# The last two steps of an attention loop in another order, with the next stage's first load a step earlier

## What is computed

```python
x = x + _L0_xattn_ref(_layernorm(x), ctx_1024, Wq, Wk, Wv, Wo, gq, gk)   # 16 heads of 128
x = x + _L0_ffn_ref(_layernorm(x), W1, b1, W2, b2, W3, b3)               # 512 -> 1024 -> 1024 -> 512
x = x + _L1_xattn_ref(_layernorm(x), ctx_1024, pos, pos, Wq, Wkv, Wout, bout)   # 32 heads of 16
x = x + _L1_ffn_ref(_layernorm(x), W_q, keys, down_embed, up_embed, gate_w, up_w, down_w)
```

```python
# _L1_xattn_ref: 16 tiles of 128 rows, each with its own 128 context rows
q = rope(x @ Wq, pos); k, v = split(ctx @ Wkv); k = rope(k, ctx_pos)
w = softmax(einsum('bqhd,bkhd->bhqk', q, k) * scale)
return einsum('bhqk,bkhd->bqhd', w, v).reshape(b, n, 512) @ Wout + bout
# _L1_ffn_ref: top 8 of 1024 experts a row by two halves of keys, beside a gated product
queries = (x @ W_q).reshape(2, n, 64); routing = einsum('tnd,tdk->tnk', queries, keys)
ew = silu(einsum('nh,nkh->nk', x, down_embed[indices])) * softmax(scores)
return silu(x @ gate_w) * (x @ up_w) @ down_w + einsum('nk,nkh->nh', ew, up_embed[indices])
```

## Time and profile before

| | |
|---|---|
| median of 3 runs | 1950.87 us (1949.71 to 1953.98) |
| the profiled execution | 1948.46 us, span 1946.7 us |
| PE busy | 1886.3 us, 97% of the span |
| DVE, ACT, POOL busy | 65%, 38%, 28% |
| granted PE clock, mean | 0.99 |
| DMA | 212.43 MB, mean 109 GB/s |

### The profile page before, as it was taken

One profiled execution on the slowest core, in us unless ns is written; L12 is line 12 of the kernel. 1 busy time (PEld: TensorE's weight loads), 2 busy tenths in 40 slices (PEclk: granted clock), 3 DMA queues, 4 the chain that ended last, 5 costly groups with the idle time before them and its releaser, 6 DMA issues. The chain is left out here.

```text
span 1946.7 us, 35580 instructions
## 1 busy us (share of the span) xinstructions
PE 1886.3 (97%) x13040; PEld 1538.1 (79%) x13040; DVE 1274.3 (65%) x2493; ACT 747.5 (38%) x2307; POOL 552.5 (28%) x702
## 2 busy tenths in 40 slices
PE   6999999999999999999999899998799999999999
PEld 5788888778888878888888677776688888888887
DVE  6666656765665655434254688886468878888786
ACT  5545555655555542211121455555332222122211
POOL 4333322222224325211021434333110222322321
PEclk9999999999999999999999999999899999999999
DMA  6453333544345433111022211112122545654554
GB/s 203 131 158 78 91 76 82 149 101 116 96 124 143 120 114 99 49 43 54 11 79 87 76 44 47 45 50 73 37 92 67 194 163 191 202 194 166 193 170 157
DMA packets 165654, 212.43 MB, mean 109 GB/s; under 512 B 29104, under 2 KB 117168, under 8 KB 165552
## 3 DMA queue, kind: packets, MB, share of 16 engines
q1 hardware_dynamic: 141840, 124.08, 23.1%
q0 software_dynamic: 23712, 87.04, 13.4%
HBM read 140.80 MB, written 17.56 MB: 81 GB/s over the span
## 5 line engine op out<-in xcount | busy, mean ns | idle before, releaser
L2421 POOL DMA_INDIRECT m_ring<-in_table,m_row x128 | 126.6, 989 | 371.4 <-DVE l_x_all L2534 265.6
L48 PE MATMUL four_banks<-l_yT_hi,m_hi 128*128 128x512 f32 x512 | 199.4, 389 | 0.0
L48 PE MATMUL four_banks<-l_yT_lo,m_hi 128*128 128x512 f32 x512 | 199.2, 389 | 0.0
L533 ACT ACTIVATE prob<-four_banks,mx,rms 128x128 f32<-128x128 f32 x256 | 121.6, 581 | 171.2 <-DVE mx L671 171.2
L1149 DVE TENSOR_SCALAR f_relu<-bank,f_b 128x512 f32<-128x512 f32 x64 | 47.9, 749 | 162.5 <-ACT f_h_hi L1092 162.4
L1092 ACT ACTIVATE f_h_hi<-bank,f_b 128x512 fp32r<-128x512 f32 x64 | 44.1, 689 | 255.1 <-PE bank L48 255.1
L335 POOL TENSOR_TENSOR rms<-ssq,constants 128x4 f32<-128x4 f32 x128 | 27.3, 214 | 394.5 <-ACT junk_k L521 277.4
L338 POOL TENSOR_TENSOR rms<-rms,constants 128x4 f32<-128x4 f32 x128 | 129.8, 1014 | 10.1
L48 PEld LDWEIGHTS four_banks<-l_yT_hi,m_hi 128*128 128x128 f32 x512 | 96.1, 188 | 20.1 <-issue 0.2
L48 PEld LDWEIGHTS four_banks<-l_yT_lo,m_hi 128*128 128x128 f32 x512 | 96.1, 188 | 19.9
L2398 ACT ACTIVATE m_act_of<-m_dot,l_ln_y 128x2 f32<-128x2 f32 x64 | 18.9, 296 | 240.6 <-DVE m_junk L2524 235.9
(11 more groups left out here) (312 smaller groups left out, 5224.6 us busy)
## 6 DMA issues: line engine op xcount, KB each, us to landing
qkT<-blocks SPq DMA_DIRECT2D x256, 128.0 KB, 2.7
pT_sb<-dealt SPq DMA_DIRECT2D x256, 64.0 KB, 2.1
f_stage<-in_w POOLq DMA_DIRECT2D x14, 512.0 KB, 4.7
f_x_in<-x SPq DMA_DIRECT2D x18, 256.0 KB, 3.2
ctx_in<-in_ctxT SPq DMA_DIRECT2D x32, 128.0 KB, 2.6
x_in<-in_x SPq DMA_DIRECT2D x16, 256.0 KB, 3.2
x<-xres SPq DMA_DIRECT2D x16, 256.0 KB, 2.9
l_rotB<-inverses SPq DMA_DIRECT2D x16, 256.0 KB
```

The lines of the kernel that those rows point to most:

```text
L48: mm = pe.matmul(out, st, mv, start=first and n == 0, stop=last and n == len(terms) - 1)
L533: a = act.activation(prob[g][:, j, :].rearrange("q (b a) -> q a b", b=4), scores, ACT.Exp, bias=mx[g][:, 1, j:j + 1], scale=rms[g][:, 0, j ...
L2421: pool.indirect_dma_start(ring[slot][:], None, table, bass.IndirectOffsetOnAxis(ap=row[:, tile_of(g), k:k + 1], axis=0)).then_inc(S[f"got{ ...
```

## The change

It moves pieces of steps 13 to 15 and of the tail; no arithmetic is added or left out.

- SP: the first load stands in step 13 behind `load_ctx(15)`, ahead of `move_maxima(14, 0)` and `store(12)`. `store(14)` goes behind `move_outputs(15)`.
- ACT: `ahead["scalar"](act, 0)` goes from the start of step 15 into step 14, ahead of `o_in(14, 1)`. `y_hi(12)` is first in step 15, `y_hi(13)` ahead of `exps(15, 1)`.
- DVE: in step 15 the splits go from the start to behind `y_lo(13)`; `y_lo(12)` is ahead of `invert(14)`, `y_lo(13)` ahead of `normalise(14)`. `spread(0)` goes from the end of step 15 behind `invert(15)`, and `layer_norm_y(14)` ahead of `normalise(15)`.
- PE: `turn_y(12)` is ahead of `score_shifted(15, 0)`; `turn_y(13)` and `route_queries(0)` are ahead of `score_shifted(15, 1)`; `mix(15)` is ahead of `output(14)`. For that it writes banks 7 and 4, not 7 and 6, and its waits and those of `output(15)` and `route_queries(1)` change.

```diff
@@ SP @@
             if there(s + 2):
                 load_ctx(sp, s + 2)
-            if there(s + 1):
-                move_maxima(s + 1, 0)
-            if there(s - 1):
-                store(s - 1)
             if isinstance(s, int) and s == NB - 3:
                 sp.wait_ge(*at("q_made", NB - 1))
                 ahead["first_load"](sp)
+            if there(s + 1):
+                move_maxima(s + 1, 0)
+            if there(s - 1) and there(s + 1):
+                store(s - 1)
...
         move_sums(NB - 1)
         move_outputs(NB - 1)
+        store(NB - 2)
         store(NB - 1)
@@ PE: mix, output, route_queries @@
+    def mix_bank(s, f):
+        return (7, 6 if there(s + 1) else 4)[f]
+
     def mix(pe, s):
         pe.wait_ge(*at("v_copied", s))
         pe.wait_ge(*at("exped1", s))
-        if there(s - 1):
+        if not there(s + 1):
+            pe.wait_ge(*at("yT_lo", SHORT + 1))
+        elif there(s - 1):
             pe.wait_ge(*at("y_added", s - 1))
...
         if there(s + 2):
             pe.wait_ge(*at("k_copied", s + 2))
+        elif there(s + 1):
+            pe.wait_ge(*at("o_in1", s))
         else:
-            pe.wait_ge(*at("o_in1", s))
+            pe.wait_ge(*at("y_added", s - 1))
...
         if c == 1:
-            pe.wait_ge(*at("yT_lo", SHORT + 1))
+            pe.wait_ge(*at("o_in1", NB - 1))
@@ PE: step @@
+            if last:
+                turn_y(pe, SHORT)
             if there(s):
                 score_shifted(pe, s, 0)
...
             if last:
-                turn_y(pe, SHORT)
+                turn_y(pe, SHORT + 1)
+                route_queries(pe, 0)
...
                 score_shifted(pe, s, 1)
             if last:
-                turn_y(pe, SHORT + 1)
-                route_queries(pe, 0)
+                mix(pe, s)
...
                 output(pe, s - 1)
...
-            if there(s):
+            if there(s) and not last:
                 mix(pe, s)
@@ ACT: o_in, step @@
-        act.activation(mixed_sb[:, f, :], bank[(7, 6)[f]][:], ACT.Copy).then_inc(S[f"o_in{f}"], 1)
+        act.activation(mixed_sb[:, f, :], bank[mix_bank(s, f)][:], ACT.Copy).then_inc(S[f"o_in{f}"], 1)
...
             if isinstance(s, int) and s == NB - 1:
-                act.wait_ge(*at("v_made", NB - 1))
-                ahead["scalar"](act, 0)
+                y_hi(act, SHORT)
...
             if isinstance(s, int) and s == NB - 1:
-                y_hi(act, SHORT)
+                y_hi(act, SHORT + 1)
...
                 exps(act, s, 1)
-            if isinstance(s, int) and s == NB - 1:
-                y_hi(act, SHORT + 1)
...
                 turned_in(act, s + 1, 1, 1)
+            if isinstance(s, int) and s == NB - 2:
+                act.wait_ge(*at("v_made", NB - 1))
+                ahead["scalar"](act, 0)
@@ DVE: step, tail @@
-            if isinstance(s, int) and s == NB - 1:
-                ahead["vector"](dve, 0)
             if there(s - 2):
                 layer_norm_y(dve, s - 2)
             if there(s + 2):
                 x_lo(dve, s + 2)
+            if isinstance(s, int) and s == NB - 1:
+                y_lo(dve, SHORT)
             if there(s - 1):
                 invert(dve, s - 1)
...
             if isinstance(s, int) and s == NB - 1:
-                y_lo(dve, SHORT)
+                y_lo(dve, SHORT + 1)
+                ahead["vector"](dve, 0)
...
-            if isinstance(s, int) and s == NB - 1:
-                y_lo(dve, SHORT + 1)
...
-            if isinstance(s, int) and s == NB - 1:
-                spread(dve, 0)
...
         invert(dve, NB - 1)
+        spread(dve, 0)
+        layer_norm_y(dve, NB - 2)
         normalise(dve, NB - 1)
-        layer_norm_y(dve, NB - 2)
         ahead["vector"](dve, 1)
```

More of the change, by code:

```diff
@@ L1630, in mix @@
                 for j in range(4):
-                    mm = pe.matmul(bank[(7, 6)[f]][PAD * j:PAD * (j + 1), t * P:(t + 1) * P], v_sb[:, 8 * t + 2 * j + f, :],
+                    mm = pe.matmul(bank[mix_bank(s, f)][PAD * j:PAD * (j + 1), t * P:(t + 1) * P], v_sb[:, 8 * t + 2 * j + f, :],
                                    probT[f][:, j, t, :], start=True, stop=True)
```

## The result

The changed kernel takes 1939.59 us (median of 5 runs, 1937.73 to 1942.84) against 1950.87 (5 runs, 1949.68 to 1953.98). The ratio is 0.9942, 95% interval 0.9931 to 0.9953: 11.3 us faster, 9.2 to 13.5. Forecast were 1943.9 us, 6.95 us faster, in a range that begins at 1940.3: right in direction, the gain too small by more than a third. Two further comparisons on other chips gave 0.9947 (0.9934 to 0.9961) and 0.9949 (0.9936 to 0.9961). The three together are 10.5 us, and 6.95 us (0.9964) lies outside each interval. The profiled execution took 1939.87 us with a span of 1938.1.

A forecast was written before the change was run, and what follows sets the result against it. PE bounds the kernel, so the gain is how much earlier `output(15)` starts: 8.35 + 0.5 - 0.3 - 0.6 - 1.0 = 6.95 us, from 1948.46 to 1941.5 profiled, 1943.9 as median; range 1940.3 to 1947.4.

The forecast's parts named there:

- part 1: Step 13: first load issued earlier on SP, so the sums of tile 13 go out sooner; gain 4.1 us.
- 0.9 us in each of two steps: SP loop: better store of the reciprocals if SP is held a little; used only for the likeliest case's range.
- is absorbed in the next: PE's waits: a clock fall starting at an earlier wait costs nothing; at `output(13)` or `output(14)` at most 2.4 us each.
- What bounds it: PE, busy 97% of the span; the change works only on about 1345 to 1405 us, the experts stage keeps the gain.
- The load behind the broadcast of tile 12, 0.3 us: Step 13: 1.5 MB issued right behind that broadcast slows it; cost 0.3 us, bounds 0 and 2.8.
- rival (a): Step 13: the load slows the broadcast of tile 12 by 2.8 us instead of 0.3; 1946.4 us, chance 0.13.
- `mix(15)` ahead of `output(14)`, 4.25 us: Step 15: mixing fills PE's wait, sums of tile 15 go out earlier; `mix(14)` to `output(15)` 28.8 us, gain 4.25 us.
- The tail, 0.5 us: After `output(15)`: full clock brings `turn_y(15)` earlier, limited by VectorE; gain 0.5 us, between 0 and 0.7.
- The clock, -1.6 us: PE clock falls cost 0.6 us at `output(13)` and 1.0 at `output(14)`, between 0 and 2.4 each.
- The maxima's write: Step 13: SP's `move_maxima(14,0)` may land up to 1 us later behind the load; `score_shifted(14,0)` has over a microsecond in hand.
- the likeliest case: Whole kernel: all parts work as summed; chance 0.68, range 1940.5 to 1946.5 us from clock terms and better reciprocal stores.
- its difference to the median, 2.4 us: Whole kernel: median of runs lies 2.4 us above the profiled execution; added to 1941.5 to give 1943.9 us.

The follow-up runs named there:

- the idle products: Kernel before, with unused products added in two of PE's waits, 20 ahead of `turn_k(15,0)` and 16 ahead of `output(15)`: ratio 0.9988, 2.3 us faster.

## Why the prediction was wrong

The prediction's own steps, in the profiles (us; two of the kernel before, three of the changed one; gains are differences of the means):

| stretch | before | changed | gain | forecast |
|---|---|---|---|---|
| `mix(12)` to `mix(13)` | 18.96, 18.56 | 18.87, 19.59, 19.43 | -0.5 | -0.3 |
| `mix(13)` to `mix(14)` | 23.23, 23.90 | 19.59, 19.54, 18.03 | 4.5 | 4.1 - 0.6 = 3.5 |
| `mix(14)` to `output(15)` | 33.11, 33.10 | 29.50, 29.54, 28.62 | 3.9 | 4.25 - 1.0 = 3.25 |
| `output(15)` to `turn_y(15)` | 11.20, 10.12 | 10.12, 10.12, 10.12 | 0.5 | 0.5 |
| `turn_y(15)` to the end | 530.15, 529.82 | 529.42, 529.66, 529.43 | 0.5 | 0 |
| together | | | 8.9 | 6.95 |

**The term that failed is the size of part 1, the load a step earlier: 4.1 us.** Its sum took 4.45 us from the odd copies to the broadcast, from the loop of tile 15. In its place in step 14 it took 3.05 us (1355.05 to 1358.10), and 3.04 to 3.05 in all ten profiles with the early load. With the load late, the same passage took 4.4 to 4.85 us in three of the four profiles and 3.07 in the fourth; what makes it short isn't shown. So the heads of tile 13 were ready 1.4 us earlier than in the sum. Where nothing else was late, the stretch took 18.0 us, as in the third profile: 5.2 to 5.9 us gained, not 4.1. Of the eight profiles with the early load and no idle products, six took 17.7 to 18.5 us. The prediction knew that this piece of the loop could be shorter (0.9 us in each of two steps) and kept it for the end of its range.

In the first two profiles another step of the prediction, wrong as well, hid that gain: that a fall of the clock "that starts at an earlier wait is absorbed in the next". The clock fell behind the wait of 1.99 us (the score products of L1616 at 1357.95 took 2.09 us, at 1372.16 at full clock 1.17). The next wait, 1 to 2.5 us ahead of `output(13)`, which should have absorbed it, was no longer there, since the heads came early. PE itself was late and reached `output(13)` 15.5 us after `mix(13)`; in the third profile it was 14.0, and by the sum 15.1.

The other steps:

- *What bounds it* was right: nearly all of the gain came out of 1350 to 1411, and the experts' stage kept it. The 0.5 us less from `turn_y(15)` to the end is in no step of the prediction. It is inside the spread of that stretch over all other versions (529.3 to 530.1 us), so it isn't shown to be the change's.
- *The load behind the broadcast of tile 12, 0.3 us*: from its issue to `normalise` 4.1 to 5.5 us in the ten profiles with the early load, mean 4.7, and 4.1 to 4.5 in the four without, mean 4.2. The price was small, about 0.5 us, and on the broadcast itself rival (a)'s 2.8 us was never reached. But in two of the ten, those of the late `spread(1)` and of the split put back, the late broadcast led to a wait of 1.7 and 1.8 us ahead of `output(12)` and the clock fell behind it; there `mix(13)` came 21.4 and 21.6 us after `mix(12)`, about what the rival had said, by another way.
- *`mix(15)` ahead of `output(14)`, 4.25 us*: from `mix(14)` to `output(15)` 28.6 us with `output(14)` at full clock, where the forecast had 28.8, and 29.5 with it at the low clock. Mechanism and size were right, the pieces less so: `output(14)` started 15.4 to 15.6 us after `mix(14)` instead of 15.0, and in the third profile the way from there was shorter by as much. Undone, it cost 6 to 7 us, not 4, because the undone state leaves longer waits than before (6.90 and 5.07 us).
- *The tail, 0.5 us*: right, and bounded by VectorE, as said: with `spread(1)` moved away it takes 8.8 us instead of 10.1.
- *The clock, -1.6 us*: against the third profile, the first two lost 1.5 us in step 14 and 0.9 behind `mix(14)`, on average over the three 1.6 us. That this equals the charge is luck: it was put on falls at `output(13)` (in none of the three) and at `output(14)` (in two). What the low clock cost the kernel before, which I had taken as all but hidden, stays open: 2.3 us by the idle products in time, with an interval from 0.6 to 4.1, and nothing by their profile.

Two smaller slips changed nothing. The maxima's write at 1347.78 was to land up to 1 us later behind the load; SP's next transfer, which waits for it, went out 3.3 us after it (1351.05), 1.9 us later than before (1347.32 to 1348.74), and PE still didn't wait. And the upper end of the likeliest case should have been 1947.1, not 1946.5: clock terms of 4.8 us instead of 1.6 take 3.2 us from the gain.

What stays open is the rest, why the timed runs give 10.5 us and the profiles 8.9. It may be no more than the spread. The profile on which the prediction rested (1948.46 us) lies below all of its 5 timed runs. I had carried its difference to the median, 2.4 us, over as a constant, which is right only if both kernels scatter alike; the first profile of the changed kernel lies 0.3 us above its median. The mean granted clock of the timed executions is 0.989 before and 0.992 after, and the clock and the time of before's executions go together (correlation -0.65 in 21 runs, about 1 us for 0.001). That points to the clock, but it isn't shown: the second profile of before has the same amount of low clock as the first, and the filled one much less without being faster.

## What to carry to other kernels

A large load belongs where nothing small stands behind it in the same queue: 1.5 MB ahead of a 16 KB transfer of sums cost 2.8 us there and 4 us at the end. When a loop's length is added up from pieces, look at all passages of a piece and not at one: what was taken as 4.45 us took 3.56 to 4.45 in the profile of before, and 3.05 after. And ask what a wait was hiding before you count on it: once the loop was shorter, the low clock that the wait would have absorbed cost 1.5 us in two of three profiles. When work is pulled forward into a wait, look at the wait that it leaves behind, and put something there too: without `mix(15)` in the gap the same moves were 6 to 7 us worse.

## What the runs showed of the hardware

- A store of 256 KB issued right behind a broadcast made its use 0.8 us later (4.46 against 3.68 us), although it was issued 0.7 us after. Over all profiles the broadcast of tile 15 took 4.2 to 4.5 us to `normalise` in the eight with the store behind it and 3.6 to 4.1 in the six without.
- The write of the reciprocals between four small copies is uneven: from the first copies to the broadcast it took 3.03, 3.05, 4.19, 4.45 and 4.81 us in the profiles, up to 5.15. Some 2.9 us of it are SP's own time to issue the five transfers (1.20, 0.57 and 1.14 us at 1355.05).
- After waits of about 2 us the granted clock fell at different places in executions of the same kernel. Behind the same 2.04 us `mix(15)` of the changed kernel took 1.96 us in two profiles and 3.28 in the third; `output(14)`, behind 2.63, 2.84 and 1.50 us, took 3.52 and 3.69 us for its first eight products in the first two and 2.11 in the third.
